# Second attention: the weights of twelve units turned by VectorE in 32x32 blocks and placed by DMA instead of transposed by TensorE

## The reference

```python
q = jnp.einsum('dc,bct->btd', Wq, init) + bq
k = jnp.einsum('dc,bct->bdt', Wk, init) + bk[None, :, None]
R = jnp.einsum('btd,bds->bts', q, k)
attention = jax.nn.softmax(R, axis=-1)
v = jnp.einsum('oc,bct->bto', Wv, x) + bv
out = jnp.einsum('bts,bsc->bct', attention, v)
```

## Time and profile before

| | |
|---|---|
| median of 3 runs | 766.23 us (765.72 to 767.99) |
| the profiled execution | 765.85 us, of which the span is 763.9 us |
| TensorE busy | 742.1 us (97%) |
| VectorE busy | 592.9 us (78%) |
| ScalarE busy | 489.2 us (64%) |
| GpSimd busy | 506.6 us (66%) |
| 540 to 580 us | TensorE 32.7, VectorE 38.1 of 40 us |
| 580 to 720 us | TensorE 139.2, VectorE 122.4, ScalarE 120.2, GpSimd 108.8 of 140 us |
| 720 to 764 us | TensorE 39.7, VectorE 26.5 of 44 us |
| granted TensorE clock | 1.00 in every stretch from 520 us on |

### The profile page before, as it was taken

The page is one execution under the profiler, slowest core; times in us unless marked ns, Lnnn a source line. Parts: engine busy times, 40 slices in busy tenths (PEclk is TensorE's granted clock), DMA queues, the critical chain, the costliest instruction groups (busy, mean ns, idle before and its releaser), DMA issues.

```text
span 763.9 us, 13606 instructions
## 1 busy us (share of the span) xinstructions
PE 742.1 (97%) x4789; PEld 590.7 (77%) x4806; DVE 592.9 (78%) x1135; ACT 489.2 (64%) x1079; POOL 506.6 (66%) x435
## 2 busy tenths in 40 slices
PE   8998999999999999999999999999879999999998
PEld 7876688888888888888888888877546777787776
DVE  5888888867788776678776666778899897898873
ACT  5756666666566545555564645447489898888773
POOL 2678676656766875556885547757577977787752
PEclk9999999999999999999999999999999999999999
DMA  9310554423454122341214301166344333122101
GB/s 345 114 69 29 132 115 99 119 84 90 112 135 109 51 98 59 92 139 60 70 32 112 86 5 28 43 231 225 83 111 105 91 91 90 35 58 71 49 15 43
DMA packets 66192, 71.10 MB, mean 93 GB/s; under 512 B 39965, under 2 KB 41469, under 8 KB 65613
## 3 DMA queue, kind: packets, MB, share of 16 engines
q1 hardware_dynamic: 65836, 69.90, 32.2%
q10 hardware_dynamic: 288, 0.33, 0.1%
HBM read 49.12 MB, written 6.34 MB: 73 GB/s over the span
## 4 chain that ended last, share of the span: by engine, by line
PE 82%; DVE 10%; ACT 3%; POOL 3%; issue 2%; DVEq 0%; POOLq 0%; ACTq 0%
PE bank L81 11%; PE bank L83 11%; PE bank L82 11%; PE bank L589 6%; PE bank L590 6%; PE bank L597 6%; PE bank L1841 4%; PE bank L662 4%; PE bank L571 3%; PE bank L1827 3%; PE bank L1795 2%; PE bank L1766 2%; PE bank L1774 2%; PE bank L1817 2%; PE bank L1818 2%
## 5 line engine op out<-in xcount | busy, mean ns | idle before, releaser
L1360 POOL TENSOR_TENSOR rope_swap<-rope_swap,trig 128x512 f32<-128x512 f32 x80 | 105.4, 1317 | 134.0 <-ACT rope_swap L754 133.8
L1054 DVE SCALAR_TENSOR_TENSOR x_res<-bank,gate,x_res 128x512 f32<-128x512 f32 x128 | 95.1, 745 | 54.6 <-PE bank L597 54.2
L589 PE MATMUL bank<-wo_hi,oT_hi 128*128 128x512 f32 x256 | 101.4, 396 | 6.8 <-DVE x_res L1054 5.5
L878 ACT CAST oT_hi<-bank 128x512 fp32r<-128x512 f32 x64 | 34.4, 589 | 111.4 <-PE bank L662 111.3
L81 PE MATMUL bank<-xnT_hi,wq_hi 128*128 128x512 f32 x252 | 101.5, 403 | 0.0
L590 PE MATMUL bank<-wo_lo,oT_hi 128*128 128x512 f32 x256 | 100.7, 393 | 0.0
L83 PE MATMUL bank<-xnT_hi,wq_lo 128*128 128x512 f32 x252 | 100.0, 397 | 0.0
L82 PE MATMUL bank<-xnT_lo,wq_hi 128*128 128x512 f32 x252 | 99.5, 395 | 0.0
L1366 POOL TENSOR_TENSOR q_rope<-rope_cos,rope_swap 128x512 f32<-128x512 f32 x64 | 82.9, 1296 | 5.0
L3175 POOL TENSOR_TENSOR b_e<-b_e,b_inv 128x512 f32<-128x512 f32 x64 | 68.3, 1082 | 19.3 <-DVE b_inv L2370 18.8
L597 PE MATMUL bank<-wo_hi,oT_lo 128*128 128x512 f32 x256 | 79.7, 394 | 0.0
(11 more groups left out here) (269 smaller groups left out, 1949.8 us busy)
## 6 DMA issues: line engine op xcount, KB each, us to landing
wq_raw<-in_wq_tiles SPq DMA_DIRECT2D x16, 512.0 KB, 3.7
wo_raw<-in_L_xattn_wo SPq DMA_DIRECT2D x16, 512.0 KB, 4.3
xn<-in_L_ffn_Wd SPq DMA_DIRECT2D x16, 256.0 KB, 2.9
b_ctx<-in_ctx SPq DMA_DIRECT2D x32, 128.0 KB, 2.6
b_k_twice<-b_qk_hi SPq DMA_DIRECT2D x32, 128.0 KB, 2.4
w_T_dram<-w_out SPq DMA_DIRECT2D x28, 128.0 KB, 3.0
w_T<-w_T_dram SPq DMA_DIRECT2D x2, 1376.0 KB, 9.2
xn<-in_L_ffn_Wg SPq DMA_DIRECT2D x10, 256.0 KB, 3.9
```

The source lines that it names most:

```text
L589: pe.matmul(out, oT_hi[:, tl, h], wo_hi[jp][:, h, :], start=(h == 0), stop=False)
L1054: dve.scalar_tensor_tensor(out=K.x[:, t, :], in0=wo_ps[t % 2][:, :], scalar=K.gate[:, 0:1], in1=K.x[:, t, :], op0=ALU.mult, op1=ALU.add).t ...
L1360: pool.tensor_tensor(out=sw, in0=sw, in1=sin_b, op=ALU.mult).then_inc(s_rope, 1)
```

## The change

For the units n = 0 and 1 (the block tb = 0) of the tiles 1 to 6, `weights_T` and `copy_T` are left out. VectorE turns the 128x512 weights in blocks of 32x32 into the one buffer `turned`, with the blocks sorted by q, the block row that they belong to (`turn_weights`). SyncE stores it to device memory (256 KB, two buffers there) and loads it back with four DMAs, each for 32 partitions of `eT[n]`, in pieces of 128 elements (`place_weights`). `attend(t, 0)` of these tiles then reads its moving side as four runs of 32 columns. A buffer `e` of such a unit is free when VectorE has turned it. `turn_weights` waits until the unit's weights are there and the store before has landed; `place_weights` waits for the transposed buffer, for the block before to be used up and for its own store. Three semaphores of the first attention are counted on. The diff, cut:

```diff
+        shared.s_probT, shared.s_p_T, shared.s_p_out = s_probT, s_p_T[0], s_p_out[0]
+        shared.n_turned, shared.n_p_T = 2 * NPAIR, 16 * ((n_quant(len(PIECES)) + 1) // 2)
+        shared.n_p_out = n_out(n_quant(len(PIECES)), 0)
...
+    M.turned, late.used = Area(cx.nc, K.late_base + late.used, 4 * D).take("b_turned", [P, D]), late.used
...
+    TURNED = range(1, NT - 1)
+
+    def turned_before(m):
+        return sum(NB * t + n < m for t in TURNED for n in range(2))
+
+    def by_pe(m):
+        return m - turned_before(m)
...
             def attend(t, tb):
-                pe.wait_ge(s_eT_sb, NB * t + 2 * tb + 2)
+                pe.wait_ge(s_eT_sb, by_pe(NB * t + 2 * tb + 2))
+                if tb == 0 and turned_before(NB * t + 2) > turned_before(NB * t):
+                    pe.wait_ge(L0.s_p_T, L0.n_p_T + 64 * turned_before(NB * t + 2))
...
-                        mm = pe.matmul(av_of(t, tb)[ch, cols], v[:, c, ch], eT[par][:, c, cols], start=(c == 0), stop=(c == DC - 1))
+                        weights = eT[par][:, c, cols]
+                        if tb == 0 and t in TURNED:
+                            weights = eT[par][:, :, c * P // 4:(c + 1) * P // 4]
+                        mm = pe.matmul(av_of(t, tb)[ch, cols], v[:, c, ch], weights, start=(c == 0), stop=(c == DC - 1))
...
-            weights_T(1, 0)
...
-            weights_T(1, 1)
...
+            def turn_weights(t, n):
+                m = NB * t + n
+                k = turned_before(m)
+                dve.wait_ge(s_w, m + 1)
+                if k:
+                    dve.wait_ge(L0.s_p_out, L0.n_p_out + 16 * k)
+                dve.transpose(M.turned[:, :].rearrange("p (q c i) -> p c q i", q=4, c=DC),
+                              e[m % 4][:, :].rearrange("p (c q i) -> p c q i", c=DC, q=4)).then_inc(L0.s_probT, 1)
...
             scale_up(2, 0)
+            turn_weights(1, 0)
             h_scales(1)
             reciprocal(1, 1)
             scale_gate(2, 1)
+            turn_weights(1, 1)
             row_max(1, 4)
...
-                after(act, s_eT, m - 3)
+                if m >= 4 and (m - 4) // NB in TURNED and (m - 4) % NB < 2:
+                    act.wait_ge(L0.s_probT, L0.n_turned + turned_before(m - 3))
+                else:
+                    after(act, s_eT, by_pe(m - 3))
...
-            copy_T(1, 0)
...
+            def place_weights(t):
+                for n in range(2):
+                    k = turned_before(NB * t + n)
+                    sp.wait_ge(L0.s_probT, L0.n_turned + k + 1)
+                    if k > 1:
+                        sp.wait_ge(L0.s_p_T, L0.n_p_T + 64 * (k - 1))
+                    sp.dma_start(K.turned_dram[k % 2], M.turned[:, :]).then_inc(L0.s_p_out, 16)
+                    if n == 0:
+                        sp.wait_ge(s_av, 4 * (t - 1) + 1)
+                    sp.wait_ge(L0.s_p_out, L0.n_p_out + 16 * (k + 1))
+                    blocks = K.turned_dram[k % 2].rearrange("(a j) (q n) -> q j a n", a=4, q=4)
+                    for q in range(4):
+                        rows = slice(q * P // 4, (q + 1) * P // 4)
+                        sp.dma_start(eT[n][rows, :, 0:P], blocks[q]).then_inc(L0.s_p_T, 16)
...
             load_ctx(4, 0)
+            place_weights(1)
             load_ctx(5, 1)
...
+    K.turned_dram = [nc.dram_tensor(f"turned_dram{i}", (P, D), F32, kind="Internal").ap() for i in range(2)]
```

More of the change, by code:

```diff
@@ L226, in n_out @@
             return sum(16 * (2 if i[4] % P else 1) for k, i in enumerate(whole) if k % 2 == b)
+        shared.s_probT, shared.s_p_T, shared.s_p_out = s_probT, s_p_T[0], s_p_out[0]
+        shared.n_turned, shared.n_p_T = 2 * NPAIR, 16 * ((n_quant(len(PIECES)) + 1) // 2)
+        shared.n_p_out = n_out(n_quant(len(PIECES)), 0)
+        tail = last_programs(cx, K, M, K.W, K.W1, shared, ctx_dram, out_dram)
         def column(p):
@@ L1616, in late_buffers @@
     M.ctx_split = two("b_ctx_split", [P, D], F32R)
+    M.logit_row = take("l1_logit_row", [P, E_ACT])
+    assert late.used <= at["q_rope1"]
     late.used = at["q_rope1"]
@@ L1623, in late_buffers @@
     M.low_w = take("l1_low", [P, DC, P + E_ACT])
-    M.logit_row = take("l1_logit_row", [P, E_ACT])
+    M.turned, late.used = Area(cx.nc, K.late_base + late.used, 4 * D).take("b_turned", [P, D]), late.used
     M.spread = take("l1_spread", [E_ALL, P])
@@ L1824, in weights_T @@
                     pe.wait_ge(M.s_w_low, 1)
-                after(pe, s_eT_sb, m)
+                after(pe, s_eT_sb, by_pe(m))
                 for c in range(DC):
@@ L2020, in tensor @@
             logits(2, 4)
-            weights_T(2, 0)
             z_T(0)
@@ L2063, in tensor @@
             logits(3, 3)
-            weights_T(3, 0)
             low(1)
@@ L2162, in tensor @@
             logits(5, 6)
-            weights_T(5, 1)
             lora(2)
@@ L2563, in vector @@
             row_max(2, 3)
+            turn_weights(2, 0)
             route_end(0)
@@ L2566, in vector @@
             residual(1)
+            turn_weights(2, 1)
             reciprocal(2, 1)
@@ L2597, in vector @@
             row_max(3, 3)
+            turn_weights(3, 0)
             row_max(3, 4)
             scale_gate(4, 0)
+            turn_weights(3, 1)
             reciprocal(3, 1)
@@ L2628, in vector @@
             make_h(4, 2)
+            turn_weights(4, 0)
             h_scales(4)
+            turn_weights(4, 1)
             finish(1)
@@ L2658, in vector @@
             row_max(5, 3)
+            turn_weights(5, 0)
             row_max(5, 4)
             scale_up(6, 0)
+            turn_weights(5, 1)
             zT_lo(2)
@@ L2693, in vector @@
             row_max(6, 3)
+            turn_weights(6, 0)
             make_h(6, 2)
@@ L2696, in vector @@
             h_scales(6)
+            turn_weights(6, 1)
             zT_lo(3)
@@ L2834, in copy_T @@
                 m, (tb, par) = NB * t + n, (n // 2, n % 2)
-                act.wait_ge(s_eT, m + 1)
+                act.wait_ge(s_eT, by_pe(m) + 1)
                 if m < 2:
@@ L2964, in scalar @@
             tanh_half(3, 1)
-            copy_T(2, 1)
             exps(2, 4)
@@ L2992, in scalar @@
             xT_copy(4)
-            copy_T(3, 0)
             exps(3, 3)
@@ L2997, in scalar @@
             x3_hi(1)
-            copy_T(3, 1)
             exps(3, 4)
@@ L3094, in scalar @@
             exps(6, 3)
-            copy_T(6, 0)
             hi_qk(7, 1)
@@ L3099, in scalar @@
             exps(6, 4)
-            copy_T(6, 1)
             exps(6, 5)
@@ L3410, in sync @@
             duplicate(3, 0)
+            place_weights(2)
             duplicate(4, 0)
@@ L3415, in sync @@
             load_ctx(6, 1)
+            place_weights(3)
             duplicate(5, 0)
             duplicate(5, 1)
+            place_weights(4)
             store(1)
@@ L3421, in sync @@
             load_ctx(7, 1)
+            place_weights(5)
             duplicate(6, 1)
@@ L3424, in sync @@
             duplicate(7, 0)
+            place_weights(6)
             store(3)
```

14 lines of the change are left out of this document (removed).

## The result

The changed kernel takes 770.25 us (median of 8 runs, 769.13 to 774.05) against 765.85 us of the kernel before, run beside it (8 runs, 764.26 to 767.99). The ratio is 1.0068, 95% interval 1.0057 to 1.0079: slower by 0.7%, some 4.4 to 5.2 us. The forecast was 770.0.

A forecast was written before the change was run, and what follows sets the result against it. The prediction took TensorE to bound the kernel, with VectorE's late releases deciding the change. Tile terms +2.0 +0.2 -0.3 +0.8 +2.2 -0.9 gave +4.0 us, median 770.2, stated as 770.0; range 764.0 to 774.5, the forecast's own 768.6 to 773.5.

The forecast's parts named there:

- the forecast's starting point, 766.23: Median of the kernel before that the prediction used; its profiled execution of 765.85 us lay 0.4 us below.
- two stalls of VectorE that were named beforehand: Tile 1: second transpose waits for the first's store, VectorE 2.5 us late; tile 5: it waits for GpSimd's weights, 3.5 us.
- Rival (a): VectorE's waits cover the transposes, so only TensorE's saving counts: 760.9 us, or 762 to 764; chance 0.12.
- Rival (b): Gains and stalls cancel within 0.3%, 2.3 us: 766 us; chance 0.28.
- Rival (c): Something unpriced is slow, the runs of 32 columns (+5 us) or the placing DMAs: 775 us and up; chance 0.12.
- TensorE's gain, 12 x 0.44 = 5.3 us: Tiles 1 to 6: twelve units lose four TensorE transposes each, 0.44 us a unit, off the binding engine.
- the 0.15 us to spare at 603.82: Tile 1: attention input xn ends at 603.67, its first TensorE matmul starts at 603.82; used against the cover holding.
- Tile 1, +2.0: The store wait makes VectorE 2.5 us late; exponential and xn come late, and TensorE leaves the tile 2.0 us late.
- Tiles 2 and 3, +0.2 and -0.3: Tile 2: two transposes, no store wait, TensorE 2.2 us late; tile 3: first covered, second waits 0.7 us, 1.9 late.
- Tile 4, +0.8: VectorE's transposes stand before the output of tile 1, for which x3_T(2) waits; TensorE's lateness becomes 2.7 us.
- Tile 5, +2.2: Second transpose waits for GpSimd's weights until 681.28; VectorE 3.5 us behind, transposes of h late, TensorE 4.9 us late.
- Tile 6, -0.9: Both VectorE transposes stand before waits, so the 0.88 us are gained; lateness falls from 4.9 to 4.0 us.

The follow-up runs named there:

- The split above: Two kernels compared: transposes and copies removed with nothing in their place (ratio 0.9956), and the changed kernel without stores and placing loads (ratio 1.0024).
- the changed kernel's second execution: The changed kernel profiled again with no edit, against the kernel before: 769.48 us, ratio 1.0056; this profiled execution took 769.03 us.

## Why the prediction was right, and where its sizes were off

**The outcome.** Slower, 770.25 us against a forecast of 770.0, within the forecast's own range. That the two agree to 0.25 us is in part luck. The terms of the sum are off by +1.1, -0.2, +0.4, +0.1, -0.6 and +0.2 us, together +1.0: the profiled execution is 5.0 us late, not 4.0, while the medians of kernel and kernel before are only 4.4 us apart, and the forecast's starting point, 766.23, lay 0.4 us above the median of the runs beside it. Nine tenths of the loss are two stalls of VectorE that were named beforehand, in tiles 1 and 5; taking both away brings the kernel level with the one before (ratio 0.9999). Rival (a), the cover holds, is wrong: TensorE waits 7.5 us (the forecast said 8 to 10). Rival (b) is outside the interval of the ratio. Rival (c) is wrong: attention's matmuls in runs of 32 columns take 272/273/324 ns (least, median, most) against 272/273/323 before, the placing loads land in 2.0 us (median), and no attention waits for them: the last load for tile 1 is issued at 593.5 and the slowest of them lands in 2.4 us, over 11 us before the attention. (The prediction's sum for it, 591.3 + 2.0 + 2.4 + 2.6, gives 598.3, not 599; nothing hangs on that.)

**TensorE's gain, 12 x 0.44 = 5.3 us.** Too large, as a saving and as busy time. With nothing in the transposes' place 3.5 us come out, and TensorE's busy time falls by 3.5 us. The prediction read 0.44 us in one place and counted it for every removed unit; in tile 1 the 0.15 us to spare at 603.82, which it used against rival (a), should have been used against this term too.

**Tile 1, +2.0, measured +3.07.** The mechanism is right, the term is mis-sized. The step "the store goes out at 586.8 and lands at 588.8" took the landing from the earlier trace rows, 2.0 us; it left on time (585.07 plus the shift of 1.68 is 586.75) and landed in 2.7. Hence a wait of 1.96 us, not 1.3, and VectorE 3.3 us late, not 2.5. The rest of the 1.07 us: the forecast let VectorE regain 0.45 us of its lateness on the way to xn (2.5 to 2.05), and it regained 0.2 (3.27 to 3.07). Removing the store wait is worth 2.07 us. The remaining 1.00 us are the two transposes on VectorE: the kernel that has them and no transfers is 1.00 us late, the kernel that has neither -0.02.

**Tiles 2 and 3, +0.2 and -0.3, measured -0.03 and +0.13.** In tile 2 the two transposes cost 0.86 us and the removed ones give 0.89. In tile 3 the transposes cost nothing, as forecast; the store wait is 0.98 us instead of 0.7, and it is not given back by other waits: without transfers the step is -0.68, and with the second transpose four steps later -0.71.

**Tile 4, +0.8, measured +0.93.** Right, on x3_T(2) behind the output of tile 1, as the wait of 1.5 us shows. The split above has 1.06 us for the transposes, 0.28 for a store wait that the forecast did not have, and -0.41 for what is gone.

**Tile 5, +2.2, measured +1.63.** The step that sets it is right: VectorE waits until GpSimd has weighed (5, 1), 2.05 us, and the whole stall costs 2.5 us less the tile's own gain. What it hits was only half right: the transposes of h wait 0.49 us, base(2) in front of them 1.56 us, for the zT part. I had that row and did not follow it to TensorE.

**Tile 6, -0.9, measured -0.74.** Right; the part without transposes on VectorE gives the same -0.75, so VectorE's work is covered there entirely.

**Unit prices.** A transpose took 0.70 us and a pitch of 0.63 as taken from the unturned ones; ScalarE is 5.6 us less busy, against the 7 that 12 copies of 0.585 make; no run shows what this is worth by itself. The Trainium skill, "VectorE: DVE Perf Modes", section "The three transpose paths", has VectorE cheaper than TensorE for a bf16 128x128 transpose, in 32x32 blocks only. In this case's float32 rows it is dearer, 0.63 against 0.44 us a unit. But the measurement also bounds what either price explains: where a tile's transposes lie in VectorE's idle time (5 and 6), the dearer engine still makes the kernel faster.

## What to carry to other kernels

Price a piece of work that is moved to another engine by its site: tile 5 made the kernel 0.85 us faster with its second transpose at one site and 1.63 us slower with it four steps earlier. Before moving work, look up at each site when its operand is ready, whether the single buffer it writes is free (the landing of a DMA, and what is ahead of that DMA in its queue), and which result of the engine directly behind it another engine needs first. When a change repeats over tiles, measure the step of each tile from a common mark: here the steps add to within 0.3 us, so the good tiles could be kept and the bad ones left out. And leave parts of a change out one by one: that split these 5.0 us into 3.6 gained on TensorE and ScalarE, 5.4 lost to VectorE's new work and 3.2 lost to waiting for stores.

## What was not expected of the hardware

The store of 256 KB landed in 2.0 us issued ahead of two context loads and in 2.7 issued behind them, while the loads took 2.5 and 2.6. So in this place the 2.0 us read elsewhere were too short for a store with two loads just ahead of it.

The two levels of the kernel before go with TensorE's granted clock early in the kernel. In its largest set of runs, 23, the twelve from 764.1 to 764.8 us have a mean granted clock of 1.000, the eleven from 765.7 to 766.3 one of 0.998. Windows of the kernel before (0.96 between 40 and 80 us), of the changed kernel's second execution (1.00), and of its first in another stretch (0.91 between 500 and 540), with the columns of the earlier trace rows:

```profile
40.00:80.00 40.00, 37.29 (x218) 28.38 (x217) 33.43 (x50) 22.65 (x56) 32.49 (x27) 0.96 0.17 57
```

```profile
40.00:80.00 40.00, 37.31 (x236) 28.64 (x236) 34.93 (x54) 23.22 (x57) 32.48 (x27) 1.00 0.17 56
```

```profile
500.00:540.00 40.00, 38.48 (x202) 30.66 (x201) 28.79 (x59) 23.49 (x56) 23.22 (x23) 0.91 0.59 218
```

A mean of 0.96 over 40 us is 1.6 us of TensorE's time, the distance of the levels (574.72 against 573.04 at the common mark). The clock falls behind a wait. In all twelve profiled executions TensorE stands still for 2.2 us, waiting for VectorE, until about 75 us. These windows are of the kernel before and of the changed kernel's second execution:

```profile
76.00:78.00 2.00, 2.00 (x6) 1.52 (x6) 1.16 (x2) 1.10 (x3) 2.00 (x2) 0.50 0.00 0
```

```profile
76.00:78.00 2.00, 2.00 (x16) 1.45 (x16) 1.73 (x3) 1.03 (x2) 2.00 (x2) 1.00 0.00 0
```

Four executions keep 1.00 between 74 and 80 us; they reach the common mark at 573.0 to 573.1. Eight are granted 0.72 to 0.74 there; seven of them reach the mark at 574.6 to 575.0, and the eighth, the changed kernel's first, at 577.6 after its second fall. The wait is the same, 2.21 to 2.23 us; why the clock falls behind it in one execution and not in the next is open.
